# Attention loop: row maxima ahead of the preceding group's row sums on VectorE

## The reference

```python
x = x + attn(cond(x, cond_128, ...), Wq, Wkv, Wo, bo)
x = x + ffn(cond2(x, cond_128, ...), w1, w3, w2, lora factors)

# attn: 32 query heads of 16 columns, 8 heads of keys and values
scores = einsum('bhqd,bhkd->bhqk', q, k)            # 32 x 32 for each sequence and head
scores = where(causal, -inf, scores)
weights = softmax(scores * 16 ** -0.5, axis=-1)
ctx = einsum('bhqk,bhkd->bhqd', weights, v)
out = ctx @ Wo + bo
```

## Time and profile before

| what | value |
| --- | --- |
| median of 3 runs | 621.25 us (620.95 to 621.43) |
| profiled execution, its own time | 623.67 us |
| its span, first to last instruction | 621.9 us |
| mean granted TensorE clock | 0.992 of full |
| busy: PE, PE weight load | 98%, 81% |
| busy: DVE, ACT, POOL | 37%, 28%, 28% |

### The profile page before, as it was taken

One profiled execution on the slowest core, in us unless ns is written; L12 is line 12 of the kernel. 1 busy time (PEld: TensorE's weight loads), 2 busy tenths in 40 slices (PEclk: granted clock), 3 DMA queues, 4 the chain that ended last, 5 costly groups with the idle time before them and its releaser, 6 DMA issues.

```text
span 621.9 us, 8095 instructions
## 1 busy us (share of the span) xinstructions
PE 610.1 (98%) x3303; PEld 501.5 (81%) x3303; DVE 227.6 (37%) x324; ACT 173.7 (28%) x295; POOL 174.6 (28%) x128
## 2 busy tenths in 40 slices
PE   9999999799999999999999999999999999999997
PEld 6988987677777788888888888798888889888885
DVE  1434553989995451111242111133111115111112
ACT  3561323566552453233111111121111111111110
POOL 3447525779998464444000000000000000000000
PEclk9999999789999999999999999999999999999999
DMA  7965655835846440000016000006100001200001
GB/s 233 357 272 198 208 194 168 250 93 158 195 142 207 164 85 0 1 1 0 1 70 134 1 0 1 1 1 175 28 0 0 0 0 51 85 0 1 0 1 67
DMA packets 36671, 55.10 MB, mean 89 GB/s; under 512 B 11392, under 2 KB 19968, under 8 KB 35392
## 3 DMA queue, kind: packets, MB, share of 16 engines
q1 hardware_dynamic: 35776, 53.29, 28.0%
q10 hardware_dynamic: 864, 1.38, 0.6%
HBM read 36.82 MB, written 16.79 MB: 86 GB/s over the span
## 4 chain that ended last, share of the span: by engine, by line
PE 84%; DVE 8%; POOL 3%; ACT 2%; DMA 1%; issue 1%; SPq 0%; DVEq 0%; ACTq 0%
PE twin L1242 39%; PE twin L1263 19%; PE twin L1084 7%; PE twin L1138 6%; POOL probs L590 3%; DVE total L919 3%; PE twin L1209 3%; PE twin L1104 2%; PE twin L1117 2%; DVE top L902 2%; ACT probs L753 2%; PE twin L1047 1%; PE twin L1195 1%; PE twin L1073 1%; DVE probs L911 1%
## 5 line engine op out<-in xcount | busy, mean ns | idle before, releaser
L988 DVE TENSOR_TENSOR gate<-twin,gate 128x512 f32<-128x512 f32 (+1 forms) x44 | 30.4, 691 | 255.5 <-PE twin L1242 255.5
L1242 PE MATMUL twin<-c_hi,f_hi 128*128 128x512 f32 (+1 forms) x352 | 96.0, 394 | 0.6 <-DVE c_lo L959 0.6
L1242 PE MATMUL twin<-c_hi,f_lo 128*128 128x512 f32 (+1 forms) x352 | 96.4, 395 | 0.0
L1242 PE MATMUL twin<-c_lo,f_hi 128*128 128x512 f32 (+1 forms) x352 | 95.7, 393 | 0.0
L1242 PEld LDWEIGHTS twin<-c_hi,f_lo 128*128 128x128 f32 (+1 forms) x352 | 65.7, 187 | 16.5
L1242 PEld LDWEIGHTS twin<-c_hi,f_hi 128*128 128x128 f32 (+1 forms) x352 | 65.2, 185 | 17.0 <-issue 1.0
L1242 PEld LDWEIGHTS twin<-c_lo,f_hi 128*128 128x128 f32 (+1 forms) x352 | 65.3, 185 | 16.1
L798 ACT ACTIVATE gate<-twin 128x512 f32<-128x512 f32 (+1 forms) x44 | 26.4, 600 | 165.9 <-PE twin L1242 165.9
L1263 PE MATMUL twin<-f_lo,gate_hi 128*128 128x512 f32 (+1 forms) x176 | 69.5, 395 | 0.0
L801 ACT CAST gate_hi<-gate 128x512 fp32r<-128x512 f32 (+1 forms) x44 | 27.3, 620 | 128.2 <-DVE gate L988 128.2
L1263 PE MATMUL twin<-f_hi_head,gate_hi 128*128 128x512 f32 x128 | 50.7, 396 | 0.0
(11 more groups left out here) (141 smaller groups left out, 813.7 us busy)
## 6 DMA issues: line engine op xcount, KB each, us to landing
f_sb<-in_f SPq DMA_DIRECT2D x2, 2752.0 KB, 19.8
x_dram<-resid_stage SPq DMA_DIRECT2D x16, 256.0 KB, 2.0
rows<-x_dram SPq DMA_DIRECT2D x16, 256.0 KB, 3.2
q_t<-q_dram SPq DMA_DIRECT2D x8, 512.0 KB, 4.3
x_dram<-rows SPq DMA_DIRECT2D x16, 256.0 KB, 2.8
near<-x_dram SPq DMA_DIRECT2D x16, 256.0 KB, 7.1
rows<-x_dram SPq DMA_DIRECT2D x4, 1024.0 KB, 6.0
out<-rows SPq DMA_DIRECT2D x16, 256.0 KB, 2.1
```

What stands on the lines that cost most here:

```text
L988: dve.tensor_tensor(gate[0:w, h % 2, :], up_bank[2 * (h % 2) + 1][0:w, :], gate[0:w, h % 2, :], ALU.mult).then_inc(gate_ready, 1)
L1242: mm = pe.matmul(bank[0:w, :], f[:, c, :], c_part[:, c, :], start=(n == 0 and c == 0), stop=(n == 2 and c == DC - 1))
```

## The change

In step 2 and all later steps of the loop, DVE's code takes the maximum of group n directly behind the transposition of group n, and the sum of group n-1 behind that. Steps 0 and 1 stay as they were. No instruction is added or removed, and the code of the other engines is the same. Behind the edit all line numbers are 2 lower (the reciprocal, L926, is L924 after the change).

```diff
-                if n == 1:
+                if due(n, 0):
                     row_tops(n)
                 if due(n, SUM):
                     m = n - SUM
                     dve.wait_ge(exp_ready, m + 1)
                     dve.tensor_reduce(total[:, m % PROBS, :], probs[:, m % PROBS], AX_X, ALU.add)\
                         .then_inc(sum_ready, 1)
-                if due(n, 0) and n != 1:
-                    row_tops(n)
                 if due(n, SUM):
                     m = n - SUM
                     dve.wait_ge(sum_ready, m + 1)
```

## The result

The changed kernel takes **622.73 us** (median of 20 executions) against 621.13 of the kernel before (20 executions): 1.60 us more, ratio 1.0026 with a 95% interval of 1.0013 to 1.0038. The forecast was 622.8, slower.

The account below looks back on a forecast made before the run. Waits through POOL and ACT and DVE's own list, almost coinciding, bound the attention loop. Groups 5 to 15 +1.59, tail +0.14, start -0.14: total +1.6 on 621.25 gives 622.8 us; range 620.9 to 623.9.

Parts of the forecast that it names:

- The bound: Attention loop, 104 to 190 us: two limits almost coincide, waits through POOL and ACT (5.46 us) and DVE's own list (5.47).
- the loop through POOL and ACT: Sum n-1, maximum n, POOL subtraction, ACT exponential, sum n: 5.46 us, holding DVE's sum about 0.12; the change cuts it.
- The price of a self-wait: DVE instruction waiting for the one just ahead costs 0.12 us: transposition to maximum 1.26, sum to reciprocal 1.25.
- The step: One group's pass through DVE's attention loop: 5.61 us after the change against 5.47, so 0.14 more.
- The start: First groups of the attention loop: second probabilities transposed at 120.21 against 120.35 us, a gain of 0.14.
- the stop: DVE waits 2.23 us for scores before transposition 5, until 129.80 us, as PE works at half clock; now until 129.66.
- The far end: From transposition 15 to the transposition of probabilities 13: 3.92 us against 3.78, +0.14; PE's gap there about 1.5.
- The self-wait is free: Rival for DVE's loop: waiting for a neighbour costs nothing, PE's 5.33 us per group decides, 2.1 faster, 619.2; chance 0.10.
- Clock at the far end: Rival: PE's clock falls after its gap before group 13's context, up to 5 us lost, 624.5 to 628; chance 0.05.
- one pair only: Rival: only one of DVE's two new neighbour pairs costs, 5.49 us per group, about +0.2, 621.4; chance 0.07.
- the start gives more: Rival: shorter gap before second context matmul brings PE's clock back sooner, saving at most 2.2 us, 620.6 to 622.3; chance 0.10.
- the next stop is shared: Before transposition 5, both kernels have DVE waiting 2.23 us for scores while PE works at half clock.

Follow-up runs that it names:

- the extra self-wait: Context remainder also waits for the end of the second transposition just ahead of it: added to the changed kernel 625.23 us, to the kernel before 621.96 us.
- the spare matmuls: Seven unread 512-column matmuls on PE ahead of each of the first two context matmuls: kernel before 620.90, changed 622.23, changed with reciprocal behind second transposition 620.30 us.
- the kernel with the older sums: Changed kernel with the reciprocal of n-1 reading the sums of n-2 and waiting for those alone, every instruction in its place: 620.72 us.

## Why the prediction was right, point by point

- **The bound.** Two limits 0.01 us apart, the loop through POOL and ACT and DVE's list with its hold. Shown by the reciprocal put next to the sum (5.80, open wait) and by the extra self-wait that costs 0.08 before and 0.23 after the change.
- **The price of a self-wait.** Taken from two pairs in the earlier trace rows, 0.12 each. In the changed profile 1.26 and 1.24 or 1.25 stand in all steps from group 6 on; taking the reciprocal's away gives 0.12 back, taking both 0.28. The maximum's is worth 0.16, as a held maximum also takes 0.04 longer. The prediction left that out, but the hold of the kernel before was 0.16 too, where it reckoned 0.12 to 0.15, so that the two errors cancel.
- **The step.** 5.61 forecast, 5.59 or 5.60 measured. Group 5 to 15: +1.59 forecast, +1.42 measured, since 5.61 was some 0.02 too long and counts ten times.
- **The start.** -0.14 forecast for the second probabilities, -0.18 measured. The prediction carried all of it through the stop; -0.04 was left. The granted clock came back in the slice from 128 and not in that from 127, so PE worked at the lower level for longer behind its second context matmul. That the total (+1.59 forecast, +1.50 measured) came out this close is in part luck: the steps were forecast 0.17 too long and the start 0.10 too good, and the two errors cancel in part.
- **The far end.** +0.14 forecast, +0.12 measured; PE's gap 1.5 forecast, 1.48 measured, clock at full.
- **The rivals.** *The self-wait is free* falls: the run with both self-waits taken away shows what that would look like, 5.31 and 619.1. With it falls, for this case, the sentence of the Trainium skill (VectorE: DVE Perf Modes, "The DRAIN you can't avoid") that the semaphore costs nothing extra: rows show 0.12, with a second semaphore 0.19. *Clock at the far end* and *one pair only* did not happen. Nor did *the start gives more*, in the profiled execution: the gap shrank to 1.38 us as forecast, but the clock came back no sooner and DVE stopped for 2.23 us again.
- **A step that was wrong, though not in the sum.** The prediction put the 2.4 us between the profiled execution and the median down to the profiler. It is the clock at the start. Own time and span of the kernel before differ by 1.7 to 1.9 us in every execution, so a span of 621.9 belongs to an own time of 623.7. Of 35 executions of the kernel before beside the spare matmuls, those with a mean granted clock of 0.996 to 0.999 took 620.06 to 621.45, those at 0.992 to 0.995 622.19 to 623.76; the profiled one had 0.992. So "the next stop is shared" holds only for executions with the long low stretch: in the profile with the reciprocal behind the second transposition, where the clock is below 1 only in the slices from 115 to 119, transposition 4 to 5 takes 5.47 with no stop. The difference survived because it is nearly the same in both kinds: +1.50 in the profiles with the stop, 1.33 between medians without it.

## What to carry to other kernels

When instructions of one engine are reordered to cut a loop through other engines, look at the new neighbours: here an instruction that waited for the one just ahead of it started behind its end and lost the overlap of 0.07 to 0.09 us that it had behind any other neighbour. The price stands in the trace of before wherever such a pair occurs even once, at the start of a pipeline for instance. And an engine without idle time may still be held: compare the distance between starts with what the same pair takes elsewhere. Here the version that keeps the maximum early and puts the reciprocal behind the second transposition is the fastest that computes the whole reference: with the spare matmuls on PE 620.30 us, against 620.90 of the kernel before and 622.23 of the changed one with the same matmuls.

## What the runs showed of the hardware that was not expected

- A self-wait on two semaphores costs more than on one, even if the second had long been fulfilled: start 0.11 us behind the neighbour's end and not 0.04 (step 5.66 against 5.59). Two semaphores alone don't do it: from group 2 on the second transposition waits for two, neither of them its neighbour's, and starts 0.08 before its neighbour ends.
- Behind the gap of 1.94 us in PE's work the granted clock fell to its lower level (1.2 of 2.4 GHz) in the profiled execution of the kernel before, in the slice from 117, more than 1.5 us before the second gap (1.92) began. Behind the gaps of 1.36 and 1.48 us at the far end of the loop it did not fall. The length of a gap alone doesn't decide: in the kernel with the older sums the clock stayed at full behind 1.88 and 2.36 us.
- How long the low stretch lasts changes from one profiled kernel to the next: 10 us in the kernel before, 3 to 4 us with the reciprocal behind the second transposition (0.50 in the slices from 116 to 118, 0.90 in those from 115 and 119), none in the one with the older sums (mean clock 1.0).
